# Rounding the phases of sequences 0 to 3 around the keeping of the last values

## The chip, the cores and the metric

One core of a Trainium2 chip runs the whole program. The metric is the time of one execution on the device in microseconds; the time before is the median of three runs. A profiled execution of the same program gives the trace. Its engines are TensorE (PE; PEld is its loading of weights), VectorE (DVE), ScalarE (ACT), GpSimd (POOL) and the DMA queue of SyncE (SP). Each engine runs its own queue of instructions in order, and semaphores order the engines among each other.

## The reference, cut to what matters

The model is a small language model tower over 8 sequences of 1024 tokens with 64 features: an embedding with a convolution, a two-layer recurrence of width 256 (most of the time), a feed-forward on the upper half of the tokens, an attention by phases, and a mixture of 8 experts. The change lies in the attention by phases:

```python
def encode(W1, b1, W2, b2):
    h = gelu(x @ W1 + b1, approximate=False)
    return tanh(h @ W2 + b2)
key_phase = encode(Wk1, bk1, Wk2, bk2) * freq * pi
query_phase = encode(Wq1, bq1, Wq2, bq2) * freq * pi
key_phasor = cos(key_phase) + 1j * sin(key_phase)
query_conj = cos(query_phase) - 1j * sin(query_phase)
V = x @ Wv + bv
memory = cumsum(key_phasor[..., None] * V[:, :, None, :], axis=1)
retrieved = real(sum(memory * query_conj[..., None], axis=2)) / sqrt(positions * K)
normed = (retrieved - mu) / sqrt(var + 1e-5) * ln_w + ln_b
return x + normed @ Wo + bo
```

freq is 1, 2, 4 or 8, so a phase can be several turns. Before a sine or cosine is taken, the kernel brings it to the nearest whole turn: it rounds the tanh output on a grid and subtracts the rounded value. The cosine is taken as the sine of a quarter turn less the absolute value.

## The kernel before, in words

All work is written out by hand, one list of instructions for each engine, with semaphores between them. Nothing plans the order: an engine does its instructions as they stand in its own block. Tokens lie as 8 sequences, each as 8 tiles of 128 tokens.

Around the change there are three stages:

- *Second norm, phases and values* (some 850 to 901 us of the span). For each sequence b, VectorE normalises it (second_in, second_variance, second_out), TensorE computes hidden phases, phases and values, ScalarE applies gelu and tanh. phase_tanh(b) (L1178) writes the tanh outputs of 64 key and 64 query phases into rph, a tile that has room for all 8 sequences. values_kept(b) (L1997) on VectorE takes the values of a sequence out of TensorE's bank and counts s_vr.
- *Attention* (some 901 to 985 us). On VectorE, rounded(b) is a tensor_scalar (L1991) into the tile whole and a tensor_tensor (L1992) that subtracts it from the own part of rph, and counts s_thr_r; the tile whole is one for all sequences. absolute(b) (L2018) writes one of two buffers rabs and counts s_abs; from sequence 2 on it waits until the sines of sequence b - 2 are done. ScalarE then takes four sines for a sequence: key cosines (L1231), key sines (L1236), query cosines (L1242) and query sines (L1244). TensorE turns the keys (keys, L1608), forms the scores (L1619) and the sums of keys by values (memory, L1629), and reads (read, L1643 and L1648); VectorE masks the scores (masked, L2026) and adds up the memory (L2034, L2036). ScalarE keeps what was read (attention_kept, L1259 and L1260), TensorE projects it (project_out, L1658 and L1662), and VectorE forms its variance (L2043) and adds it to the rows (add_out, L2048 to L2052).
- *Experts* (from 985 us on).

Between the first two stages stands one small side chain. VectorE's L2054 writes lnb, the normalisation's bias spread over a tile, and counts s_lnb. TensorE waits for it (after s_vr = 8) and multiplies it by the output weights in two small matmuls (L1668, L1669), ahead of keys(0). ScalarE waits for those, copies the row (L1263), and only behind this copy, in its own queue, stand the sines of sequence 0:

```python
act.wait_ge(s_row_b, 1)
act.activation(cwb[:, :], bank[6][:, D:2 * D], ACT.Copy).then_inc(s_row_k, 1)
for b in range(2):
    key_cosines(b)
```

VectorE's order before the change is: the loop over the second norm, values_kept(7), lnb (L2054), rounded(0), absolute(0), rounded(1), absolute(1), masked(0), memory(0), and then the loop over b, which for b < 6 begins with rounded(b + 2) and absolute(b + 2) (with three small blocks of the third norm and the gates ahead of them at b = 4, 6 and 7).

Of the kernel before, what the change touches and what calls it, by code (L numbers as in the profile page):

```python
# [7 lines left out]
ALU = mybir.AluOpType  # L8
# [4 lines left out]
I32 = mybir.dt.int32  # L13
# [4 lines left out]
B, T = 8, 1024  # L18
# [73 lines left out]
def build(nc, a, out, kept):  # L92
    with ExitStack() as ctx:
# [3 lines left out]
        def sem(name):  # L97
            return ctx.enter_context(nc.semaphore(name))
# [13 lines left out]
        def wide_sums(layer, s):  # L112
# [80 lines left out]
        s_kq, s_kqg, s_ph, s_th, s_thr_r, s_v, s_vr = (  # L193
            sem(n) for n in ("kq_hidden", "kq_gelu", "kq_phase", "kq_tanh", "phase_kept", "values_summed", "values_kept"))
        s_abs, s_phk, s_phi, s_s, s_sm, s_k, s_kt, s_st, s_mem, s_att, s_rt = (
            sem(n) for n in ("phases_absolute", "key_phasors", "phasors", "scores", "scores_masked", "keys_turned",
                             "keys_copied", "memory_added", "memory_summed", "attention_summed", "attention_kept"))
# [100 lines left out]
        def tokens(x):  # L298

            return x.rearrange("p (t d) -> p t d", t=TT)  # L300
# [589 lines left out]
        rph = hi_space.bitcast(F32)  # L890
# [25 lines left out]
        rabs = lo2[:, 0:2048].rearrange("p (q t) -> p q t", q=2)  # L916
# [908 lines left out]
        def _(dve):  # L1825
# [143 lines left out]
            def second_in(b):  # L1969
                dve.wait_ge(s_ytr, 5 + b // 2)  # L1970
                link(dve.tensor_tensor(tmp8[:, :, :], yw[:, span(b), :],
                                       weigh[:, span(b)].unsqueeze(2).to_broadcast([P, TT, D + 1]), ALU.mult))
                dve.tensor_tensor(xc2[:, b % 2, :, :], tmp8[:, :, :], res[:, span(b), :], ALU.add).then_inc(s_xc, 1)

            def second_variance(b):
                dve.wait_ge(s_sq, b + 1)
                dve.reduce_sum(rstd_row(b, 0), sq[:, :, :], AX.X).then_inc(s_var, 1)

            def second_out(b):
                dve.wait_ge(s_rstd, b + 1)  # L1980
                if b:
                    dve.wait_ge(s_xs, OPEN + b)
                dve.tensor_tensor(nrm[:, :, :], xc2[:, b % 2, :, 0:D], spread(rstd_row(b, 2)), ALU.mult).then_inc(s_nrm, 1)
                dve.wait_ge(s_nrm, b + 1)
                dve.tensor_tensor(res[:, span(b), :], xc2[:, b % 2, :, :], nrmw[:, :, :], ALU.add)
                norm_low(dve, b)

            def rounded(b):
                own = rph[:, b * T:(b + 1) * T]
                dve.wait_ge(s_th, 2 * b + 2)  # L1990
                link(dve.tensor_scalar(whole[:, :], own, column(GRID), column(GRID), ALU.add, ALU.subtract))  # L1991
                dve.tensor_tensor(own, own, whole[:, :], ALU.subtract).then_inc(s_thr_r, 1)  # L1992

            dve.wait_ge(s_fcb, 1)
            def values_kept(b):
                dve.wait_ge(s_v, b + 1)
                dve.tensor_scalar(vv[:, span(b), :], tokens(bank[4][:, :]), inv[:, S_V:S_V + 1], None,  # L1997
                                  ALU.mult).then_inc(s_vr, 1)
# [4 lines left out]
            for b in range(B):  # L2003
                if b + 1 < B:
                    second_variance(b + 1)
                second_out(b)
                if b + 2 < B:
                    second_in(b + 2)
                if b:
                    values_kept(b - 1)  # L2010
            values_kept(B - 1)


            def absolute(b):
                if b >= 2:
                    dve.wait_ge(s_phi, b - 1)
                dve.wait_ge(s_thr_r, b + 1)
                dve.tensor_scalar(rabs[:, b % 2, :].bitcast(I32), rph[:, b * T:(b + 1) * T].bitcast(I32), 0x7FFFFFFF, None,  # L2018
                                  ALU.bitwise_and).then_inc(s_abs, 1)

            def masked(b):
                if b >= 2:
                    dve.wait_ge(s_att, b - 1)
                for half in range(2):
                    dve.wait_ge(s_s, b * 2 + half + 1)
                    dve.tensor_tensor(sm[:, b % 2, half * 4:half * 4 + 4, :],  # L2026
                                      bank[2 + half][:, :].rearrange("p (t k) -> p t k", t=4),
                                      tri[:, :].unsqueeze(1).to_broadcast([P, 4, P]), ALU.mult).then_inc(s_sm, 1)
# [17 lines left out]
            def add_out(b):  # L2046
                own, part = res[:, span(b), 0:D], tmp8[:, :, 0:D]
                link(dve.tensor_tensor(own, own, rows(cwb[:, :]), ALU.add))  # L2048
                dve.wait_ge(s_rs, b + 1)
                dve.tensor_tensor(part, tokens(bank[7][:, :]), spread(stat[:, 7, :]), ALU.mult).then_inc(s_wor, 1)  # L2050
                dve.wait_ge(s_wor, b + 1)
                link(dve.tensor_tensor(own, own, part, ALU.add))  # L2052
# [4 lines left out]
            def third_mean(x):  # L2057
                link(dve.reduce_sum(stat[:, 0, :], res[:, span(x), 0:D], AX.X))

            def third_centre(x):  # L2060
                dve.wait_ge(s_nrm, B + x)
                dve.scalar_tensor_tensor(xc[:, :, :], spread(stat[:, 0, :]), -1.0 / D, res[:, span(x), 0:D], ALU.mult,
                                         ALU.add).then_inc(s_xc, 1)
# [10 lines left out]
            def third_low(x):  # L2074
                dve.wait_ge(s_xh, B + x + 1)
                dve.tensor_tensor(xs3_by[1], by_half(nrm[:, :, :]), xs3_by[0], ALU.subtract).then_inc(s_xs, 1)
# [12 lines left out]
            def gate_greater(x):  # L2089
                dve.wait_ge(s_rank, x + 1)  # L2090
                link(dve.tensor_tensor(gdiff[:, :, :, :], gdiff[:, :, :, :],
                                       order[:, :, :].unsqueeze(1).to_broadcast([P, TT, NE, NE]), ALU.is_gt))

            def gate_rank(x):
                link(dve.reduce_sum(grank[:, :, :], gdiff[:, :, :, :], AX.X))
                link(dve.tensor_scalar(gsel[:, :, :], grank[:, :, :], 1.5, None, ALU.is_lt))

            def gate_weights(x):
                dve.wait_ge(s_ex, x + 1)
                link(dve.tensor_tensor(gc[:, :, :], gex[:, :, :], gsel[:, :, :], ALU.mult))  # L2100
                link(dve.reduce_sum(gst[:, 1, :], gc[:, :, :], AX.X))
                link(dve.reciprocal(gst[:, 2, :], gst[:, 1, :]))
                if x:
                    dve.wait_ge(s_wgt_t, x)
                dve.tensor_tensor(gleft[:, 0:NE, :].rearrange("p e t -> p t e"), gc[:, :, :], per(gst[:, 2, :]),
                                  ALU.mult).then_inc(s_wgt, 1)

            for b in range(2):
                rounded(b)
                absolute(b)  # L2110
            masked(0)
            memory(0)
            dve.wait_ge(s_row_k, 1)
            for b in range(B):
                if b == 4:
                    third_low(0)
                elif b == 6:
                    gate_greater(0)
                    gate_rank(0)
                    gate_weights(0)  # L2120
                elif b == 7:
                    third_low(1)
                if b < B - 2:
                    rounded(b + 2)
                    absolute(b + 2)
                if b < B - 1:
                    masked(b + 1)
                if b:
                    add_out(b - 1)
                if b == 1:  # L2130
                    third_mean(0)
                    third_centre(0)
                elif b == 2:
                    third_variance(0)
                elif b == 3:
                    third_scale(0)
                    third_mean(1)
                elif b == 4:
                    third_centre(1)
                elif b == 5:  # L2140
                    third_variance(1)
                    gate_logits(0, bank[6][:, D:2 * D])
                elif b == 6:
                    third_scale(1)
                elif b == 7:
                    third_mean(2)
                    third_centre(2)
                if b < B - 1:
                    memory(b + 1)
                variance_of(b)  # L2150
# [28 lines left out]
            for n in range(slots):  # L2179
                b, e = divmod(n, NE)  # L2180
# [119 lines left out]
```

## Time and profile before

| | us |
|---|---|
| median of three runs (lowest, highest) | 1123.51 (1123.03, 1123.75) |
| profiled execution | 1123.85 |
| its span | 1122.0 |
| PE busy | 1061.1 (95%) |
| ACT busy | 769.2 (69%) |
| DVE busy | 686.4 (61%) |
| POOL busy | 147.4 (13%) |

The timeline counts in microseconds from the start of the span. A row of it has the start, the time of the instruction or of a merged group of them, the engine, the line of the program, the operation, what it writes and reads, and how many instructions the row holds. In brackets is idle time of that engine just before, and what ended it. In the table by windows, PEclk is the granted clock of TensorE as a share of the full 2.4 GHz; 0.50 is 1.2 GHz.

### The profile page before, as it was taken

How to read it: one execution, taken by the hardware profiler on the slowest of the kernel's cores; microseconds unless marked ns; L12 is line 12 of the kernel's file. 1: busy time of each engine (PE TensorE's matmuls, PEld its weight loads, DVE VectorE, ACT ScalarE, POOL GpSimd, SP SyncE). 2: the span in 40 equal slices, each digit the busy share in tenths (PEclk: the TensorE clock that was granted, in tenths of full speed). 3: DMA queues.
4: the chain of work that ended last, by engine and by line, in shares of the span. 5: the costliest groups of instructions: out<-in, count | busy, mean ns of one | idle time of the engine just before them, and what ended most of it. 6: DMA issues, size and time to landing. Idle time of an engine off the chain costs nothing.

```text
span 1122.0 us, 62678 instructions
## 1 busy us (share of the span) xinstructions
PE 1061.1 (95%) x26978; PEld 859.2 (77%) x26978; DVE 686.4 (61%) x3132; ACT 769.2 (69%) x4585; POOL 147.4 (13%) x220
## 2 busy tenths in 40 slices
PE   4799999999999999999999999999899879889998
PEld 2688899999999999999999999999744368833332
DVE  7566455555555555555555544444456758899996
ACT  1466677777767777777777776666567888667664
POOL 4300000011000100000110000000003402341320
PEclk9699999999999999999999999898699989999999
DMA  5000000000000000000000000000000000167786
GB/s 147 7 10 9 9 9 15 9 10 9 9 11 13 9 9 9 10 14 9 9 5 5 4 5 5 5 4 5 3 1 1 1 2 1 29 240 249 277 294 209
DMA packets 30642, 47.29 MB, mean 42 GB/s; under 512 B 12298, under 2 KB 21651, under 8 KB 30364
## 3 DMA queue, kind: packets, MB, share of 16 engines
q1 hardware_dynamic: 29820, 43.15, 11.5%
q8 instruction: 211, 3.46, 1.2%
q14 instruction: 67, 0.55, 0.2%
q10 hardware_dynamic: 544, 0.13, 0.1%
HBM read 40.88 MB, written 2.39 MB: 39 GB/s over the span
## 4 chain that ended last, share of the span: by engine, by line
PE 80%; DVE 9%; ACT 5%; issue 3%; DMA 2%; POOL 1%; SPq 0%; DVEq 0%; ACTq 0%; POOLq 0%
PE bank L680 44%; PE bank L777 7%; PE bank L671 5%; PE bank L760 4%; PE bank L441 3%; PE bank L540 2%; PE bank L1750 2%; PE bank L1696 2%; DMA space<-weights_kept 1%; PE bank L1437 1%; PE bank L1470 1%; PE bank L755 1%; DVE space L2159 1%; PE bank L1619 1%; PE bank L772 1%
## 5 line engine op out<-in xcount | busy, mean ns | idle before, releaser
L680 PE MATMUL bank<-space,whh_hi 128*128 128x32 f16 (+1 forms) x16384 | 574.0, 175 | 8.3 <-DVE space L808 4.4
L680 PEld LDWEIGHTS bank<-space,whh_hi 128*128 128x128 f16 x16384 | 481.9, 96 | 71.1 <-DVE space L808 8.0
L808 DVE TENSOR_TENSOR space<-h_f,space 128x16 f16<-128x16 f32 x2048 | 284.6, 176 | 365.5 <-ACT h_f L789 360.9
L789 ACT ACTIVATE h_f<-bank 128x16 f32<-128x16 f32 x2048 | 293.4, 184 | 226.4 <-PE bank L680 220.3
L795 ACT ACTIVATE space<-bank 128x16 f16<-128x16 f32 x2048 | 292.6, 184 | 1.1 <-PE bank L680 1.1
L671 PE MATMUL bank<-space,whh_lo 128*128 128x32 f16 (+1 forms) x2096 | 131.4, 177 | 0.0
L777 PE MATMUL bank<-space,wih_hi 128*128 128x32 f16 x2048 | 129.1, 177 | 0.0
L760 PE MATMUL bank<-xr,wih_hi 128*128 128x32 f16 x512 | 97.4, 190 | 0.0
L441 PE MATMUL bank<-onehot,tab 128*128 128x128 f16 x448 | 95.5, 219 | 0.5 <-DVE prepare_cur L491 0.5
L755 PE MATMUL bank<-ones,bias 128*128 128x32 bf16 x512 | 91.7, 179 | 0.0
L671 PEld LDWEIGHTS bank<-space,whh_lo 128*128 128x128 f16 x2096 | 90.1, 96 | 0.0
L777 PEld LDWEIGHTS bank<-space,wih_hi 128*128 128x128 f16 x2048 | 87.7, 96 | 0.0
L760 PE MATMUL bank<-xr,wih_lo 128*128 128x32 f16 x512 | 70.6, 193 | 0.0
L361 POOL TENSOR_SCALAR prepare_stat<-prepare_stat 128x2 f32<-128x2 f32 x28 | 6.1, 218 | 478.9 <-DVE prepare_stat L356 478.9
L777 PE MATMUL bank<-space,wih_lo 128*128 128x32 f16 x1024 | 64.5, 177 | 0.0
L772 PE MATMUL bank<-ones,bias 128*128 128x32 bf16 x512 | 52.9, 179 | 0.0
L1696 PE MATMUL bank<-xt,wx 64*128 64x512 f16 (+1 forms) x390 | 48.1, 375 | 2.3 <-ACT gel L1299 1.5
L760 PEld LDWEIGHTS bank<-xr,wih_hi 128*128 128x128 f16 x512 | 49.9, 98 | 0.0
L1299 ACT ACTIVATE space<-bank,ebias 128x1024 f32<-128x1024 f32 x31 | 33.6, 1110 | 23.1 <-PE bank L1696 23.1
L755 PEld LDWEIGHTS bank<-ones,bias 128*128 128x128 bf16 x512 | 49.2, 96 | 0.0
L760 PEld LDWEIGHTS bank<-xr,wih_lo 128*128 128x128 f16 x512 | 45.1, 96 | 0.0
L777 PEld LDWEIGHTS bank<-space,wih_lo 128*128 128x128 f16 x1024 | 43.8, 96 | 0.0
(309 smaller groups left out, 1598.9 us busy)
## 6 DMA issues: line engine op xcount, KB each, us to landing
space<-weights_kept SPq DMA_DIRECT2D x64, 512.0 KB, 7.8
space<-in_x SPq DMA_DIRECT2D x28, 129.0 KB, 3.1
out<-res SPq DMA_DIRECT2D x7, 256.0 KB, 9.8
space<-in_wrec SPq DMA_DIRECT2D x1, 768.0 KB, 4.3
space<-in_wx SPq DMA_DIRECT2D x1, 744.5 KB, 8.9
weights_kept<-wturned SPq DMA_DIRECT2D x8, 36.0 KB
whole<-weights_kept SPq DMA_DIRECT2D x8, 36.0 KB
brec<-in_brec SPq DMA_DIRECT2D x1, 260.0 KB
```

The costliest lines, as they stand in the source:

```text
L441: mm = pe.matmul(P_CONV[:, b * P:(b + 1) * P], tab[part][:, v, tap, :], onehot[:, m % 2, v, b, tap:tap + P], start=(n == 0), stop=(n == 7) ...
L671: mm = pe.matmul(own[:, m, :], w[:, k, m * P:(m + 1) * P], steps(h, k), start=False, stop=False, skip_group_check=True)
L680: mm = pe.matmul(own[:, m, 0:copies, :], w[:, k, m * P:(m + 1) * P], state[:, k, :].unsqueeze(1).to_broadcast([P, copies, B]), start=False ...
L755: pe.matmul(own, bias[:, m * P:(m + 1) * P], ones[:, 0:U * B], start=(m == 0), stop=False, skip_group_check=True)
L760: pe.matmul(own.rearrange("p s b -> p b s"), (wih0_hi, wih0_lo)[part - 1][:, m * P:(m + 1) * P], xr[:, :, n * U:(n + 1) * U], start=False, ...
L772: pe.matmul(own, bias[:, H + m * P:H + (m + 1) * P], ones[:, 0:U * B], start=(m == 0), stop=False, skip_group_check=True)
L777: pe.matmul(own, w[:, k, m * P:(m + 1) * P], h[0][:, k, at:at + U, part, :], start=False, stop=False, skip_group_check=True)
L789: act.activation(h_f[layer][:, s % 2, :, :], own, ACT.Tanh, scale=scale[layer]).then_inc(s_h[layer], 1)
L795: act.activation(h[layer][:, :, s % RINGS[layer], 0, :], own, ACT.Tanh, scale=scale[layer]).then_inc(s_hi[layer], 1)
L808: dve.tensor_tensor(h[layer][:, :, s % RINGS[layer], 1, :], h_f[layer][:, s % 2, :, :], h[layer][:, :, s % RINGS[layer], 0, :], ALU.subtra ...
L1299: act.activation(expert_at(n), banks[n % 2 * 2][:, :], ACT.Relu, bias=ebias[:, n % NE:n % NE + 1], scale=unscale[S_E1]).then_inc(s_r, 1)
L1696: mm = pe.matmul(own[:, half * 512 + at:half * 512 + at + count], wx[w][rows, W_E1 + e * HE:W_E1 + (e + 1) * HE], xt[rows, bass.ds(b * T + ...
```

## The change

In the program after, rounded(0), absolute(0), rounded(1) and absolute(1) are issued between values_kept(6) and values_kept(7). rounded(2) and rounded(3) are issued right behind values_kept(7), ahead of lnb. In the loop rounded(b + 2) is left for b + 2 of 4 or more, and absolute(b + 2) stays where it was. rounded(b) has a further wait: from sequence 1 on it waits until the subtraction of the sequence before is done, since the tile whole is shared. The same instructions are executed as before; there are seven waits more.

```diff
             def rounded(b):
                 own = rph[:, b * T:(b + 1) * T]
                 dve.wait_ge(s_th, 2 * b + 2)
+                if b:
+                    dve.wait_ge(s_thr_r, b)
                 link(dve.tensor_scalar(whole[:, :], own, column(GRID), column(GRID), ALU.add, ALU.subtract))
                 dve.tensor_tensor(own, own, whole[:, :], ALU.subtract).then_inc(s_thr_r, 1)
+
+            def absolute(b):
+                if b >= 2:
+                    dve.wait_ge(s_phi, b - 1)
+                dve.wait_ge(s_thr_r, b + 1)
+                dve.tensor_scalar(rabs[:, b % 2, :].bitcast(I32), rph[:, b * T:(b + 1) * T].bitcast(I32), 0x7FFFFFFF, None,
+                                  ALU.bitwise_and).then_inc(s_abs, 1)
...
                 if b:
                     values_kept(b - 1)
+            for b in range(2):
+                rounded(b)
+                absolute(b)
             values_kept(B - 1)
-
-
-            def absolute(b):
...
+            rounded(2)
+            rounded(3)
+
...
-            for b in range(2):
-                rounded(b)
-                absolute(b)
             masked(0)
             memory(0)
             dve.wait_ge(s_row_k, 1)
...
                 if b < B - 2:
-                    rounded(b + 2)
+                    if b + 2 >= 4:
+                        rounded(b + 2)
                     absolute(b + 2)
```

The line that writes lnb (L2054 before) is not touched; it stands between the two changed places.

## Rows read from the trace of the kernel before

**Rows 1.** The page: the chain that ended last, by engine.

```profile
PE 80%; DVE 9%; ACT 5%; issue 3%; DMA 2%; POOL 1%; SPq 0%; DVEq 0%; ACTq 0%; POOLq 0%
```

**Rows 2.** Timeline of VectorE from 894 to 927 us.

```profile
894.72 0.75 DVE L1997 TENSOR_SCALAR xr<-bank,inv 128x512 f32<-128x512 f32 x1
900.69 0.75 DVE L1997 TENSOR_SCALAR xr<-bank,inv 128x512 f32<-128x512 f32 x1 [5.22 <-PE bank L1447]
901.36 0.28 DVE L2054 TENSOR_SCALAR space<-ones,col 128x128 f32<-128x128 f32 x1
901.55 0.81 DVE L1991 TENSOR_SCALAR whole<-space,col 128x1024 f32<-128x1024 f32 x1
902.39 1.22 DVE L1992 TENSOR_TENSOR space<-space,whole 128x1024 f32<-128x1024 f32 x1
903.65 0.69 DVE L2018 TENSOR_SCALAR space<-space 128x1024 int32<-128x1024 int32 x1
904.26 0.81 DVE L1991 TENSOR_SCALAR whole<-space,col 128x1024 f32<-128x1024 f32 x1
...
916.51 0.81 DVE L1991 TENSOR_SCALAR whole<-space,col 128x1024 f32<-128x1024 f32 x1
917.35 1.22 DVE L1992 TENSOR_TENSOR space<-space,whole 128x1024 f32<-128x1024 f32 x1
918.68 0.69 DVE L2018 TENSOR_SCALAR space<-space 128x1024 int32<-128x1024 int32 x1
...
926.61 1.51 DVE L2026 TENSOR_TENSOR gel<-bank,tri 128x512 f32<-128x512 f32 x2 [0.41 <-PE bank L1619]
```

**Rows 3.** Timeline of ScalarE from 884 to 921 us.

```profile
884.08 1.10 ACT L1178 ACTIVATE space<-bank,col 128x1024 f32<-128x1024 f32 x1
...
902.73 0.22 ACT L1263 ACTIVATE space<-bank 128x64 f32<-128x64 f32 x1
904.38 1.24 ACT L1231 ACTIVATE space<-space,col 64x1024 f32<-64x1024 f32 x1 [1.42 <-DVE space L2018]
...
914.01 1.15 ACT L1244 ACTIVATE space<-space,col 64x1024 f32<-64x1024 f32 x1
...
919.41 1.24 ACT L1231 ACTIVATE space<-space,col 64x1024 f32<-64x1024 f32 x1 [3.04 <-DVE space L2018]
920.55 0.67 ACT L1259 ACTIVATE ntb<-bank,col 128x512 f32<-128x512 f32 x1
```

**Rows 4.** Timeline of TensorE from 901 to 926 us.

```profile
901.73 0.19 PE L1668 MATMUL bank<-bias,ones 128*128 128x64 bf16 x1 [1.08 <-DVE space L2054]
901.85 0.43 PE L1669 MATMUL bank<-wobd,space 64*128 64x64 f32 x2
906.83 1.97 PE L1608 MATMUL bank<-eye,space 128*128 128x128 f32 x8 [4.54 <-ACT space L1236]
909.25 3.79 PE L1619 MATMUL bank<-space 128*128 128x128 f32 x16 [0.45 <-ACT space L1244]
...
914.63 1.04 PE L1608 MATMUL bank<-eye,space 128*128 128x128 f32 x8
915.52 1.95 PE L1619 MATMUL bank<-space 128*128 128x128 f32 x16
...
918.98 0.38 PE L1648 MATMUL bank<-space,gp 128*64 128x128 f32 x2
...
925.35 2.05 PE L1619 MATMUL bank<-space 128*128 128x128 f32 x16 [1.20 <-ACT space L1244]
```

**Rows 5.** Busy time of each engine by window, attention loop; columns: window, length, engines.

```profile
926.60:951.20 24.60, 23.62 (x244) 22.11 (x242) 23.05 (x50) 19.84 (x23) 5.97 (x5) 1.00 0.00 1
```

**Rows 6.** The same view; the third number from the end is PEclk.

```profile
901.00:903.00 2.00, 0.55 (x3) 0.39 (x3) 1.97 (x4) 1.89 (x4) 0.00 (x0) 1.00 0.00 0
903.00:905.00 2.00, 0.00 (x0) 0.00 (x0) 1.97 (x3) 0.62 (x1) 0.00 (x0) 0.55 0.00 0
...
913.00:915.00 2.00, 2.00 (x19) 2.00 (x18) 0.86 (x2) 1.99 (x2) 0.00 (x0) 0.89 0.00 0
```

More of the change, by code:

```diff
@@ L2010, in _ @@
                     values_kept(b - 1)
+            for b in range(2):
+                rounded(b)
+                absolute(b)
             values_kept(B - 1)
-            def absolute(b):
[L2015 to L2019, printed above, removed]
+            rounded(2)
+            rounded(3)
             def masked(b):
```

## The prediction

> **What bounds the kernel now.** The profiled execution took 1123.85 us, 1.85 us of it outside its span of 1122.0 us; the median of the three timed runs is 1123.51 us, 0.34 us less. I count a shift of the end against the profiled execution and then apply it to the median.
>
> I read the chain of waits first. TensorE carries 80% of it, but that is an average over stages [rows 1]. The change touches 30 us of 1122, the passage from the second norm and phases into the attention loop, so only the timelines of that passage count. Four facts decide.
>
> First, VectorE has a hole: after it has kept the values of sequence 6 at 894.72 us it waits 5.22 us for TensorE's last value projection and goes on at 900.69 [rows 2].
>
> Second, VectorE then has a queue of its own: the small lnb instruction (L2054, 901.36), two rounds of 0.81 + 1.22 us with an absolute value of 0.69 us behind each, ending at 907. ScalarE's first cosine (L1231) starts at 904.38, right after the first absolute value ends at 904.34; before it lie 1.42 us of idle time [rows 2, 3].
>
> Third, a side chain goes through lnb: lnb (901.36) feeds the two row matmuls on TensorE (L1668, 901.73; L1669, ending 902.28), and ScalarE's copy of that row, L1263 at 902.73, stands ahead of the first cosine in ScalarE's queue. Before the change it is early by the 1.42 us of idle time and costs nothing [rows 3, 4].
>
> Fourth, in the loop ScalarE waits 3.04 us for the absolute value of sequence 2, which stands behind a round that starts at 916.51. Further on VectorE is busy nearly without a pause (23.05 of 24.6 us) from its first masking of sequence 2 at 926.61, and what it waited for there was scores(2) on TensorE, which in turn waited 1.20 us for ScalarE's sines (L1244) [rows 2 to 5]. Later cosines wait for VectorE too, so a shift of 926.61 goes through to the end as it is: all four engines hang on each other from there, and nothing in the last stages is tied to an absolute time.
>
> **The change part by part.**
>
> *Rounds 0 and 1 with their absolute values go into the hole.* The tanh outputs are there: that of sequence 3, the latest used ahead of the loop, starts at 884.08 and takes 1.10 us [rows 3]. A round occupies 0.84 + 1.26 us (901.55 to 902.39 to 903.65), an absolute value 0.61 (903.65 to 904.26) [rows 2]: 2.71 us for a sequence, 5.42 for two. The instruction after a keeping starts 0.67 us after it (900.69 to 901.36), so they run from 895.39 to 900.81. The keeping of the last values starts there, 0.12 us later than before. TensorE and ScalarE cover these 5.3 us. Nothing is paid, and 5.4 us of VectorE's queue behind 901.4 are gone.
>
> *Rounds 2 and 3 go between that keeping and lnb.* Here I look at what they are moved ahead of: lnb is the next instruction after them. Count on: the keeping ends its slot at 901.48. Round 2 takes 0.84 and then 1.33, because round 3 now waits for its end through two semaphores: with two waits the step behind such a subtraction is 1.33 (917.35 to 918.68), with one 1.26 [rows 2]. That is 903.65. Round 3 takes 0.84 and about 1.15 (no wait behind it; an estimate from 1.22 less the 0.08 by which instructions without a wait overlap, 903.65 to 904.26 for one of 0.69), so lnb starts at 905.64 instead of 901.36, 4.28 us late.
>
> From there: lnb's start to the end of the row matmuls was 0.92 us (902.28 less 901.36) [rows 2, 4]. They would now start at 905.64 + 0.37 = 906.01 (901.36 to 901.73), and TensorE has had nothing since 900.65 (901.73 less its 1.08 us of waiting): 5.4 us of idle time. The row of the stretch from 903 shows the granted clock falling from 2.4 to 1.2 GHz (0.55) once the engine stood still [rows 6], and eight transposes at the low level take 1.97 us against 1.04 at the high one [rows 4]. So the 0.55 us of row matmuls become at most 1.1; I take 0.25 us more. They end at 906.81 (bounds 906.56 and 907.11). ScalarE's copy follows in 0.04 and the cosine 0.25 after it (0.22 us of work and a gap of 0.03): 907.10 instead of 904.38. **The first cosine is 2.72 us late**, bounds 2.5 and 3.0. The absolute values, ready since 898 and 901, no longer matter.
>
> *What that does to sequences 0 and 1.* ScalarE's eight sines, keys_kept, TensorE's keys(0), scores(0), memory(0), keys(1) and scores(1) hang one on the other without slack, so they shift by 2.72. If TensorE's full clock came back a little earlier in this sequence, scores(1) could gain at most the 0.3 us by which it now starts (915.52) later than ScalarE's last sine of sequence 1 allows (914.01 + 1.15) [rows 3, 4].
>
> *What round 2 gives back.* Round 2 is no longer in front of absolute value 2. VectorE reaches it at 916.51 + 2.72 = 919.23 instead of 918.68, so cosine 2 starts 0.55 us late instead of 2.72. But the next instruction of ScalarE, the keeping of the attention output (L1259), needs read(0), whose last matmul ended at 918.98 + 0.38 = 919.36. ScalarE could have started at 919.40 and did at 920.55: only 1.15 us of slack in ScalarE's lateness are there to be recovered [rows 3, 4]. Read(0) now ends 2.72 later, so L1259 starts at 922.12, and the shift from here is 2.72 - 1.15 = **1.57 us**. On TensorE, project_out(0), keys(2) and scores(2) come to less (scores(2) waited 1.20 us for ScalarE), so ScalarE's sines set it.
>
> *What round 3 gives back: nothing.* It leaves a stretch in which VectorE had to wait anyway (0.41 us in front of 926.61, released by TensorE's L1619) [rows 2]. That wait becomes some 2 us longer. Rounds 4 to 7 stay where they are.
>
> *The added wait on s_thr_r.* For rounds 1 and 2 the semaphore has long arrived, for round 3 it is counted above. For rounds 4 to 7 it is a second wait in a part where VectorE sets the pace: between 0 and 0.07 us each, 0.28 in all; I take 0.08 in all, since other long instructions (0.69 us) cover such a wait. The one observation is 1.33 against 1.26 us. The Trainium skill (VectorE: DVE Perf Modes, section "The DRAIN you can't avoid") says that a semaphore after each operation costs nothing over one after the last. By it the sum is 0.15 us smaller in all; by the row, up to 0.2 larger.
>
> Sum: 2.72 - 1.15 + 0.08 = 1.65 us. On the profiled execution that is 1125.5 us, on the median **1125.2 us**.
>
> **The rivals.**
>
> *A. TensorE's full clock comes back after keys(1) and scores(1).* Before, the clock was at the high level again in the stretch from 913 (0.89 on average), just ahead of keys(1) at 914.63 [rows 4, 6]. With everything 2.7 us later and a few row matmuls alone in the middle of the idle time, it may still be low when keys(1) begins. Price: eight transposes 1.97 against 1.04, sixteen score matmuls 3.79 against 1.95 [rows 4], together 2.8 us on the chain: 1.65 + 2.8 = 4.4, so 1127.9 us, slower. It decides when the low stretch outlasts scores(0) and memory(0). For it: such short bursts did not raise the clock before. Against: keys(0) and scores(0) come just as dense as before, and they shift with the rest. The Trainium skill (TensorE: Matmul & The Clock Gate, "What's actually happening") says that the clock follows recent activity at moments that don't restart with the kernel; by that the stretch can be longer or shorter than a rigid shift makes it, which is why A has a chance at all.
>
> *B. VectorE paces the loop from its first pass on.* Then both rounds taken out of the loop would be paid back: 2.72 - 2 x 2.10 + 0.08 = -1.4, so 1122.1 us. Against it stands the 0.41 us that VectorE waited for TensorE before 926.61 [rows 2].
>
> *C. The side chain is not late*, because something else than I read orders lnb. Then the first cosine follows the row copy at 902.73 + 0.25 = 902.98, 1.40 us earlier, and the 1.15 us come on top: -2.55, so 1121.0 us. The order of the code speaks against it.
>
> *D. Slack that I did not see swallows the delay*, in the passage from attention to the experts: 1123.5 us. The dense stretch [rows 5] speaks against it.
>
> **How the numbers follow.** Forecast 0.67, A 0.14, D 0.09, B 0.06, C 0.04. A difference under 0.2% (2.25 us) can't be told from none. The forecast has its own range, 1.1 to 2.3 us and a tail, so some 0.08 of it lies over 2.25; with A that is 0.22 for slower. Faster: C and a little of B, 0.05. The rest, 0.73, is within 0.2%: a loss of 0.15% by mechanism, but too small for a verdict. The forecast's own range is 1124.5 to 1125.9; to leave no more than 0.2 outside, the range goes from 1122.9 (D in, B and C out) to 1127.0 (the shorter cases of A in).
>
> **What would show it.** Right: in the profile after, rounds 0 and 1 at 895.4 to 900.8; lnb near 905.6; the row matmuls behind it at the low clock; the copy L1263 near 906.8 and the first cosine near 907.1 with a wait on TensorE instead of VectorE; cosine 2 near 920.0; L1259 near 922.1; first masking of sequence 2 near 928.2; everything behind 1.6 us late. Wrong: a first cosine before 905, scores(1) taking over 3 us (A), or VectorE without idle time in front of the masking of sequence 2 (B).

## The result, and the profile after

The changed kernel took 1124.85 us, the median of 22 runs (1123.44 to 1126.29), against 1122.98 us for the kernel before in 22 runs of its own beside it (1122.12 to 1125.32). The ratio is 1.0016, 95% interval 1.0009 to 1.0022: 1.8 us slower (1.0 to 2.5), within the 0.2% that can hardly be told from none. The forecast was 1.65 us slower.

The profiled execution after took 1126.29 us with a span of 1124.5 us. Its passage from the norm to the attention starts 0.28 us earlier than in the one before (the last tanh, L1178, at 899.79 instead of 900.07 us), so shifts within the passage are counted from that tanh. VectorE's timeline after (rounded is now L1993 and L1994, absolute L2000, values_kept L2006, lnb L2061, masked L2033) answers to [rows 2]:

```profile
895.11 0.80 DVE L1993 TENSOR_SCALAR whole<-space,col 128x1024 f32<-128x1024 f32 x1
...
899.92 0.69 DVE L2000 TENSOR_SCALAR space<-space 128x1024 int32<-128x1024 int32 x1
900.53 0.74 DVE L2006 TENSOR_SCALAR xr<-bank,inv 128x512 f32<-128x512 f32 x1
901.19 0.80 DVE L1993 TENSOR_SCALAR whole<-space,col 128x1024 f32<-128x1024 f32 x1
902.02 1.22 DVE L1994 TENSOR_TENSOR space<-space,whole 128x1024 f32<-128x1024 f32 x1
903.36 0.81 DVE L1993 TENSOR_SCALAR whole<-space,col 128x1024 f32<-128x1024 f32 x1
904.21 1.23 DVE L1994 TENSOR_TENSOR space<-space,whole 128x1024 f32<-128x1024 f32 x1
905.35 0.28 DVE L2061 TENSOR_SCALAR space<-ones,col 128x128 f32<-128x128 f32 x1
...
917.55 0.69 DVE L2000 TENSOR_SCALAR space<-space 128x1024 int32<-128x1024 int32 x1
...
927.66 1.52 DVE L2033 TENSOR_TENSOR gel<-bank,tri 128x512 f32<-128x512 f32 x2 [1.87 <-PE bank L1619]
```

Rounds 0 and 1 with their absolute values fill the hole from 895.11 on; the last keeping starts at 900.53, 0.12 us later in the passage than before (900.69 less 0.28). Then two rounds stand in front of lnb, which starts at 905.35 instead of 901.36. In front of the masking at 927.66 VectorE now waits 1.87 us for TensorE, where it waited 0.41.

ScalarE, which answers to [rows 3]; the first row is the last tanh:

```profile
899.79 1.11 ACT L1178 ACTIVATE space<-bank,col 128x1024 f32<-128x1024 f32 x1 [0.56 <-PE bank L1527]
...
906.65 0.22 ACT L1263 ACTIVATE space<-bank 128x64 f32<-128x64 f32 x1 [4.23 <-PE bank L1669]
906.77 1.23 ACT L1231 ACTIVATE space<-space,col 64x1024 f32<-64x1024 f32 x1
...
916.39 1.14 ACT L1244 ACTIVATE space<-space,col 64x1024 f32<-64x1024 f32 x1
...
918.67 1.24 ACT L1231 ACTIVATE space<-space,col 64x1024 f32<-64x1024 f32 x1
921.58 0.69 ACT L1259 ACTIVATE ntb<-bank,col 128x512 f32<-128x512 f32 x1 [1.66 <-PE bank L1648]
```

The copy of the row, L1263, has 4.23 us of idle time in front of it, released by TensorE's row matmul, and the first cosine follows it directly. Before, ScalarE waited for the absolute value (L2018); now this wait is gone and the one for the side chain stands in its place. TensorE, which answers to [rows 4]:

```profile
905.87 0.69 PE L1669 MATMUL bank<-wobd,space 64*128 64x64 f32 x2
909.22 1.97 PE L1608 MATMUL bank<-eye,space 128*128 128x128 f32 x8 [2.66 <-ACT space L1236]
911.63 2.70 PE L1619 MATMUL bank<-space 128*128 128x128 f32 x16 [0.45 <-ACT space L1244]
...
915.68 1.04 PE L1608 MATMUL bank<-eye,space 128*128 128x128 f32 x8
917.59 2.05 PE L1619 MATMUL bank<-space 128*128 128x128 f32 x16 [0.87 <-ACT space L1244]
...
921.16 0.38 PE L1648 MATMUL bank<-space,gp 128*64 128x128 f32 x2
```

The two f32 row matmuls take 0.69 us instead of 0.43: they ran at the low clock (PEclk 0.50 from 905 to 907). The sixteen score matmuls of sequence 0 took 2.70 us instead of 3.79, because the clock came back within them (0.50 from 911 to 913, 1.00 from 913 to 915). The last row is the end of read(0), at 921.54.

Counted from the last tanh, the first cosine comes at 6.98 us (before 4.31, so 2.67 late), the first attention output L1259 at 21.79 (before 20.48, 1.31 late). From there to the seventh L1259 the shift stays at 1.31 to 1.32 us. At the eighth something new appears. The last tanh and the last L1259 on ScalarE's timeline of the execution before:

```profile
900.07 1.11 ACT L1178 ACTIVATE space<-bank,col 128x1024 f32<-128x1024 f32 x1 [0.56 <-PE bank L1527]
...
981.87 0.69 ACT L1259 ACTIVATE ntb<-bank,col 128x512 f32<-128x512 f32 x1 [3.11 <-PE bank L1648]
```

and the last L1259 after:

```profile
984.28 0.69 ACT L1259 ACTIVATE ntb<-bank,col 128x512 f32<-128x512 f32 x1 [4.49 <-PE bank L1648]
```

TensorE's first matmuls of read(7), before:

```profile
979.86 0.51 PE L1643 MATMUL bank<-gel,xr 128*64 128x128 f32 x5 [1.20 <-issue]
```

and after:

```profile
980.89 0.51 PE L1643 MATMUL bank<-gel,xr 128*64 128x128 f32 x5 [1.20 <-issue]
```

The windows around read(7) (PEclk is the third number from the end), before:

```profile
980.00:982.00 2.00, 2.00 (x34) 1.71 (x35) 1.05 (x2) 0.13 (x1) 1.94 (x1) 1.00 0.93 274
982.00:984.00 2.00, 2.00 (x24) 1.58 (x20) 1.89 (x3) 2.00 (x4) 0.00 (x0) 1.00 0.92 350
```

and after:

```profile
980.00:982.00 2.00, 1.10 (x14) 1.14 (x16) 1.90 (x7) 0.00 (x0) 1.05 (x1) 0.82 0.85 281
982.00:984.00 2.00, 2.00 (x20) 1.84 (x16) 0.97 (x3) 0.00 (x0) 0.97 (x1) 0.50 0.81 328
984.00:986.00 2.00, 2.00 (x19) 1.12 (x18) 1.87 (x3) 1.72 (x3) 0.00 (x0) 0.83 0.95 381
```

After the change TensorE ran most of read(7) at 0.50, that is at 1.2 GHz, where it had 2.4 GHz before. Ahead of it the engine had stood idle for 1.2 us in both executions. The view names no releaser (issue); by the program and VectorE's timeline it waited for the memory sums, which end 0.1 us before read(7) starts. The clock was still full in that pause and fell some 0.4 us after the matmuls had resumed (0.78 on average from 981.0 to 981.5, 0.50 from there). First to last L1259 is 61.32 us before and 62.70 after: that fall of the clock costs 1.4 us, which is why this one execution is 2.4 us over the one before and not 1.0.

### The profile page after: what moved, and what is told of

Same layout as the page of the kernel before. It is cut to its first block, busy times and chain, and to the rows that moved or that the text cites. A ratio compares the mean times of both kernels' runs of the same rounds, so it can differ in the third digit from the quotient of the medians.

```text
span 1124.5 us, 62684 instructions
## 1 busy us (share of the span) xinstructions
PE 1060.7 (94%) x26978; PEld 860.7 (77%) x26978; DVE 688.2 (61%) x3132; ACT 770.1 (68%) x4585; POOL 146.0 (13%) x220
## 4 chain that ended last, share of the span: by engine, by line
PE 82%; DVE 9%; ACT 5%; issue 3%; POOL 1%; DMA 0%; SPq 0%; DVEq 0%; ACTq 0%; POOLq 0%
PE bank L680 44%; PE bank L777 7%; PE bank L671 5%; PE bank L760 4%; PE bank L1750 3%; PE bank L441 2%; PE bank L540 2%; PE bank L1696 2%; PE bank L1437 1%; PE bank L1470 1%; PE bank L755 1%; PE bank L772 1%; PE bank L1619 1%; DVE space L1994 1%; PE bank L426 1%
```

## The experiments

Theory L: the change loses because lnb, 4.3 us late, delays the first cosine; round 2 gives back a part, round 3 nothing. Rival K: the loss is the clock of TensorE, which fell once more. Rival W: the added waits cost it. Medians scatter: the same kernel timed twice gave 0.9969 (6 runs) and 0.9982 (12 runs), 1.5 us apart. The parts that the change leaves alone scatter as much: in the fourteen traces the last tanh starts between 898.89 and 900.45 us, and from the last L1259 to the end of the span it is 139.4 to 142.2 us. So the timelines of the passage decide beside the medians. All places are counted from the start of the last tanh, in us, in the one profiled execution of each kernel; ratios are to the kernel before, timed beside each:

| kernel | ratio (95%) | first cosine | first L1259 | last L1259 | first to last |
|---|---|---|---|---|---|
| before | | 4.31 | 20.48 | 81.80 | 61.32 |
| changed | 1.0016 (1.0009 to 1.0022) | 6.98 | 21.79 | 84.49 | 62.70 |
| changed, again | 1.0019 (1.0010 to 1.0028) | 6.98 | 21.93 | 83.24 | 61.31 |
| lnb ahead | 0.9969 (0.9956 to 0.9981) | 2.78 | 18.01 | 80.88 | 62.87 |
| lnb ahead, again | 0.9982 (0.9973 to 0.9990) | 2.78 | 17.95 | 80.79 | 62.84 |
| only rounds 0 and 1 moved | 0.9988 (0.9979 to 0.9997) | 2.79 | 18.84 | 80.15 | 61.31 |
| round 3 back | 0.9992 (0.9983 to 1.0001) | 4.52 | 19.32 | 80.64 | 61.32 |
| lnb ahead, round 3 back | 0.9985 (0.9976 to 0.9993) | 2.78 | 18.06 | 80.96 | 62.90 |
| before, lnb late | 1.0029 (1.0017 to 1.0041) | 8.14 | 23.08 | 85.64 | 62.56 |
| changed, filled at read(7) | 1.0012 (1.0003 to 1.0021) | 6.98 | 21.78 | 83.10 | 61.32 |
| before, filled at read(7) | 0.9998 (0.9988 to 1.0009) | 4.31 | 20.54 | 81.84 | 61.30 |
| lnb ahead, filled at read(7) | 0.9983 (0.9974 to 0.9992) | 2.78 | 17.62 | 78.96 | 61.34 |
| lnb ahead, filled at both | 0.9980 (0.9971 to 0.9989) | 2.78 | 17.59 | 78.94 | 61.35 |
| lnb ahead, filled at keys(0) | 0.9985 (0.9975 to 0.9995) | 2.78 | 17.58 | 79.47 | 61.89 |

**lnb ahead of rounds 2 and 3.** One line of the changed kernel moves:

```diff
             values_kept(B - 1)
+            dve.tensor_scalar(lnb[:, :], ones32[:, :], column(LN_B), None, ALU.mult).then_inc(s_lnb, 1)
             rounded(2)
             rounded(3)
...
-            dve.tensor_scalar(lnb[:, :], ones32[:, :], column(LN_B), None, ALU.mult).then_inc(s_lnb, 1)
```

> The changed kernel with one line moved: lnb is written right behind values_kept(7), ahead of rounds 2 and 3. Theory L (the late side chain through lnb costs 2.7 us at the first cosine, and only that makes the change lose): lnb near 901.5, row copy near 902.7, first cosine near 903.0 instead of 904.4 before, so 1.4 us early, and the 1.15 us of slack in front of L1259 come on top: 2.5 us under the kernel before (between 1.5 and 2.9), some 4 us under the changed kernel. Rival K (the loss comes from TensorE's clock, which fell once more in the changed kernel's profiled execution, at read(7)): moving the line changes little, still 1 to 2 us over the kernel before. Rival W (the seven added waits cost it): still slower than the kernel before.

Measured: 1119.86 against 1123.56 us, ratio 0.9969: 3.5 us less by the ratio, more than the expected 1.5 to 2.9. ScalarE's timeline of this kernel, from the last tanh on:

```profile
899.83 1.11 ACT L1178 ACTIVATE space<-bank,col 128x1024 f32<-128x1024 f32 x1 [0.56 <-PE bank L1527]
...
902.49 0.22 ACT L1263 ACTIVATE space<-bank 128x64 f32<-128x64 f32 x1
902.61 1.23 ACT L1231 ACTIVATE space<-space,col 64x1024 f32<-64x1024 f32 x1
...
915.66 1.24 ACT L1231 ACTIVATE space<-space,col 64x1024 f32<-64x1024 f32 x1 [0.86 <-DVE space L2000]
917.84 0.69 ACT L1259 ACTIVATE ntb<-bank,col 128x512 f32<-128x512 f32 x1 [0.93 <-PE bank L1648]
```

The first cosine stands 1.53 us nearer to the last tanh than before and the first L1259 2.47. That is the expected 2.5. K and W expected a loss; the sign turned with one line, though this kernel has all seven added waits and its trace has the fall of the clock at read(7) too (first to last 62.87). Theory L stands.

**Only rounds 0 and 1 moved.** Rounds 2 and 3 go back into the loop, `if b + 2 >= 4` becomes `>= 2`:

> The changed kernel with rounds 2 and 3 back in the loop; only rounds 0 and 1 with their absolute values stand in the hole, and lnb follows values_kept(7) directly. Theory L: first cosine 1.4 us early, and everything behind it shifts rigidly, 1.4 us under the kernel before (0.9 to 1.8). It is then 1.1 us over the kernel with lnb ahead and rounds 2 and 3 behind it, which is what round 2 gives back. Rival K: as far over the kernel before as the changed kernel, 1 to 2 us. Rival W: the same, since the waits are still there.

```profile
900.45 1.11 ACT L1178 ACTIVATE space<-bank,col 128x1024 f32<-128x1024 f32 x1 [0.56 <-PE bank L1527]
...
903.24 1.23 ACT L1231 ACTIVATE space<-space,col 64x1024 f32<-64x1024 f32 x1
...
918.14 1.24 ACT L1231 ACTIVATE space<-space,col 64x1024 f32<-64x1024 f32 x1 [3.04 <-DVE space L2000]
919.29 0.67 ACT L1259 ACTIVATE ntb<-bank,col 128x512 f32<-128x512 f32 x1
```

Ratio 0.9988, by it 1.3 us under before. The first cosine is as early as with lnb ahead, and the 3.04 us of waiting for absolute value 2 are back in front of 918.14. The first L1259 comes 0.83 us later than with lnb ahead (18.84 against 18.01). That is what moving round 2 is worth once lnb is not behind it. I had expected 1.1; the rest lies in scores(1), which starts 13.80 us after the last tanh here and 14.12 with lnb ahead (914.25 and 913.95 in the two timelines), 0.32 us later, and 0.83 + 0.32 is 1.15.

**Round 3 back in the loop**, round 2 still ahead of lnb (`rounded(3)` ahead of the loop deleted, `>= 4` becomes `>= 3`):

> The changed kernel with round 3 back in the loop, round 2 still ahead of lnb. Theory L: lnb is 2.1 us earlier than in the changed kernel (near 903.5), first cosine near 904.9, half a microsecond later than before the change, less 1.15 us of slack: 0.6 us under the kernel before (0 to 1.2), 2 us under the changed kernel. If instead round 3 ahead of the loop gave something back, this would lose part of it: it would be less than 1.5 us under the changed kernel. Rival K: no clear difference from the changed kernel.

```profile
899.62 1.11 ACT L1178 ACTIVATE space<-bank,col 128x1024 f32<-128x1024 f32 x1 [0.56 <-PE bank L1527]
...
904.02 0.22 ACT L1263 ACTIVATE space<-bank 128x64 f32<-128x64 f32 x1 [1.77 <-PE bank L1669]
904.14 1.23 ACT L1231 ACTIVATE space<-space,col 64x1024 f32<-64x1024 f32 x1
...
916.17 1.24 ACT L1231 ACTIVATE space<-space,col 64x1024 f32<-64x1024 f32 x1 [0.17 <-DVE space L2000]
918.94 0.69 ACT L1259 ACTIVATE ntb<-bank,col 128x512 f32<-128x512 f32 x1 [1.52 <-PE bank L1648]
```

Ratio 0.9992 (0.9983 to 1.0001), where the changed kernel has 1.0016: 2.7 us less by taking one round from in front of lnb. The first cosine is 2.46 us earlier than in the changed kernel, and L1259 2.47 (19.32 against 21.79). Against the kernel before it is 0.9 us less by the ratio and 1.16 at L1259, where 0.6 (0 to 1.2) was expected: the cosine came 0.21 us late and not half a microsecond.

**lnb ahead, round 3 back in the loop**, to see round 3's worth without its cost:

> lnb ahead of round 2, round 3 back in the loop. The prediction's step that round 3 gives nothing back: VectorE waits in front of the masking of sequence 2 in either case, so L1259 and that masking come as in the kernel with lnb ahead of rounds 2 and 3 (18.0 and 24 us after the last tanh), and the time is the same within 0.5 us. If round 3 ahead of the loop were worth something, this would be slower by up to 2.1 us.

The first masking of sequence 2 on VectorE's timeline, with lnb ahead of rounds 2 and 3:

```profile
923.92 1.52 DVE L2034 TENSOR_TENSOR gel<-bank,tri 128x512 f32<-128x512 f32 x2 [1.87 <-PE bank L1619]
```

and with round 3 back in the loop:

```profile
924.13 1.29 DVE L2033 TENSOR_TENSOR gel<-bank,tri 128x512 f32<-128x512 f32 x2
```

From the last tanh these are 24.09 and 24.36 us. With the round in the loop the 1.87 us of waiting are filled, and the masking is 0.27 us late; its two halves then follow without a gap (1.29 instead of 1.52 us), so it ends at about the same place. L1259 comes at 18.06 and 18.01. The ratios are 0.9985 and, with lnb ahead, 0.9982 timed beside it (0.9969 the first time). Round 3 ahead of the loop is worth nothing on the path.

**lnb late alone**, in the kernel before: the line that writes lnb goes behind absolute(1):

> The kernel before with one line moved: lnb is written behind absolute(1) instead of ahead of rounded(0), all rounds where they were. Theory L, the cost alone: lnb starts near 907.0 instead of 901.4 (5.6 us late, of which 1.4 fall into ScalarE's old idle time), first cosine near 908.4 instead of 904.4. Round 2 is still in the loop and shifts with the rest, so nothing is given back: 3.6 to 4.0 us over the kernel before. If the side chain did not matter: no difference.

```profile
899.40 1.11 ACT L1178 ACTIVATE space<-bank,col 128x1024 f32<-128x1024 f32 x1 [0.56 <-PE bank L1527]
...
907.42 0.22 ACT L1263 ACTIVATE space<-bank 128x64 f32<-128x64 f32 x1 [5.39 <-PE bank L1669]
907.54 1.23 ACT L1231 ACTIVATE space<-space,col 64x1024 f32<-64x1024 f32 x1
...
921.33 1.24 ACT L1231 ACTIVATE space<-space,col 64x1024 f32<-64x1024 f32 x1 [1.92 <-DVE space L2018]
922.48 0.67 ACT L1259 ACTIVATE ntb<-bank,col 128x512 f32<-128x512 f32 x1
```

Ratio 1.0029 (1.0017 to 1.0041), 3.3 us slower where 3.6 to 4.0 was expected; the first cosine is 3.83 late. But at L1259 only 2.60 are left, so "nothing is given back" was wrong by 1.2 us. TensorE's full clock came back within scores(0) (2.81 us for the sixteen matmuls, 3.79 before), memory(0) ended earlier in the sequence, and with it round 2, which follows it on VectorE, and cosine 2.

**Filled at read(7).** Five matmuls on TensorE into a free bank, whose result is not used, keep it running through the 1.2 us in front of read(7), in three kernels:

```diff
+                if b == B - 1:
+                    pe.wait_ge(s_sm, 2 * B)
+                    for i in range(5):
+                        pe.matmul(bank[2][:, :], eye16[:, :], xt[:, 0:512], start=True, stop=True,
+                                  skip_group_check=True)
                 read(b)
```

> The changed kernel with five extra matmuls of 512 columns on TensorE into a free bank, just ahead of read(7), where TensorE has 1.2 us of idle time while it waits for the memory sums; their result is not used. Rival K (the clock fell to 1.2 GHz at read(7) in the changed kernel's profiled execution and cost 1.4 us there, and such falls are a good part of the measured loss): at full clock through read(7), and 1.2 to 1.4 us over the kernel before, with less spread between runs. Theory L alone: the same 1.8 us over the kernel before as without the extra matmuls, or a little more if they hold read(7) up.

> The kernel before with the five extra matmuls ahead of read(7). Control for the clock: if falls of the clock at read(7) also happen in the kernel before, in a part of its runs, it is 0.1 to 0.5 us faster and less spread than the kernel before; if they don't, or if the extra matmuls cost something, between 0 and 0.3 us slower.

> The kernel with lnb ahead of rounds 2 and 3, with the five extra matmuls ahead of read(7). Its profiled execution without them showed a fall of the clock at read(7) and the last attention output 1.5 us later than a rigid shift. Theory K for this spot: full clock through read(7), the last L1259 80.2 to 79.3 us after the start of the last tanh, and the median equal to that of the kernel without them or up to 1.4 us lower, depending on how often the fall happened in its timed runs; against the kernel before 2.5 to 4.5 us less. If the fall costs nothing: no difference.

In the timelines the fill does what it should: first to last L1259 is 61.3 us in all four kernels that have it. Of the ten traces without it five show the fall at read(7) and 62.6 to 62.9 us. (The tenth is the kernel filled at keys(0) alone, below.) The medians don't show it: 1.0012 against 1.0016 and 1.0019, 0.9998 for the kernel before, and 0.9983 where lnb ahead alone had 0.9969 and 0.9982. The changed kernel with the fill is 1.3 us over before, where K put it, but the interval (0.3 to 2.4) holds L's 1.8 as well, and its runs spread more (1123.39 to 1127.51) and not less. With lnb ahead the fill came out at 1.9 us under before, outside the expected 2.5 to 4.5, which is a miss. One place where that execution lost time can be read. From its last L1259 to the end of the span it took 142.2 us, against 139.4 to 140.8 in the other thirteen traces (139.6 in that of lnb ahead). The view of the waits has VectorE's waits for the expert weights' DMA in that execution (us in total, times, longest):

```profile
DVE gel L2169 <- DMA space<-weights_kept: 7.9, 5, 4.0
```

and in the one of lnb ahead:

```profile
DVE gel L2164 <- DMA space<-weights_kept: 5.4, 4, 2.7
```

So VectorE waited 2.5 us more for DMAs there. Whether all of that lay on the path isn't shown. The kernel filled at both places finished its attention as early and had 4.5 us of these waits and 139.7 us to the end, so the early finish alone does not bring it about; chance is likely, and not shown.

**Filled at keys(0) as well, and there alone.** Twelve such matmuls into bank 5 behind the row matmuls:

```diff
                       skip_group_check=True).then_inc(s_row_b, 1)
+            for i in range(12):
+                pe.matmul(bank[5][:, :], eye16[:, :], xt[:, 0:512], start=True, stop=True, skip_group_check=True)
```

> The same, and twelve more extra matmuls of 512 columns behind the row matmuls, in the idle time ahead of keys(0) (2.9 us), so that TensorE keeps running. If the clock stays at 2.4 GHz, keys(0) and scores(0) take 1.0 and 2.0 us instead of 1.8 and 3.8. On the path only 0.6 us can come of it, since scores(1) then waits for ScalarE's last sine of sequence 1 (in the kernel with lnb ahead it started at 913.95, the sine ended at 913.37): 0.3 to 0.6 us less than with the fill ahead of read(7) alone. If the low clock were a main cost of this passage, it would be 2 us or more.

> lnb ahead of rounds 2 and 3, and only the twelve extra matmuls ahead of keys(0). The clock stays up through keys(0) and scores(0) as in the kernel with both fills. L1259 comes 17.6 us after the last tanh against 18.0 without: 0 to 0.6 us less than lnb ahead alone, too little to be told in the median. A gain of over 1.5 us would mean that the low clock costs more than the path says.

TensorE of the kernel filled at both places:

```profile
904.90 1.09 PE L1608 MATMUL bank<-eye,space 128*128 128x128 f32 x8 [0.20 <-ACT space L1236]
907.32 2.05 PE L1619 MATMUL bank<-space 128*128 128x128 f32 x16 [1.33 <-ACT space L1244]
...
913.28 2.05 PE L1619 MATMUL bank<-space 128*128 128x128 f32 x16 [1.31 <-ACT space L1244]
```

keys(0) takes 1.09 and scores(0) 2.05 us, both at the full clock. Nevertheless L1259 comes at 17.59 and 17.58 where the four traces with lnb ahead and no fill here have 18.01, 17.95, 18.06 and 17.62: 0.0 to 0.5 us for some 2.4 us of TensorE time saved (keys(0) and scores(0) take 3.14 us together, 5.57 with lnb ahead), since scores(1) then waits 1.31 us for ScalarE's last sine. Against the kernel filled at read(7) alone it is only 0.03 us in the traces, less than the expected 0.3 to 0.6: there keys(0) and scores(0) ran at the low clock (1.97 and 3.78 us), and scores(1) still started only 0.14 us later after the last tanh (13.74 against 13.60). In the median it can't be told (0.9980 and 0.9985, 0.9983 with the fill at read(7) alone). In the kernel filled at keys(0) alone the clock fell at another place, near 967.8 us, 1.8 us into matmuls that ran without a pause behind one of 0.79 us; the seventh L1259 came late by it, and of the pause in front of read(7) only 0.16 us were left, so that first to last grew by 0.6 us (61.89).

**Twice more.** The changed kernel and the one with lnb ahead once more:

> The changed kernel once more, for a second profiled execution. Shift of L1259 from the start of the last tanh: 21.8 us, as in the first (20.5 in the kernel before), since the order sets it. The fall of the clock at read(7) is open: if it is tied to where this kernel's TensorE idles, it is there again and the last L1259 comes 84.5 us after the last tanh; if it is chance, it may be missing and that is 83.1. Time 1.3 to 2.7 us over the kernel before.

> The kernel with lnb ahead of rounds 2 and 3 once more, since its first timing (3.5 us under the kernel before) is larger than the timelines give (2.5 us at L1259). If the timelines are right, 2.0 to 3.0 us under the kernel before, and where the clock falls at read(7) 1.5 us less than that. If something else in the kernel gives a further 1 us, 3.5 again.

```profile
982.13 0.69 ACT L1259 ACTIVATE ntb<-bank,col 128x512 f32<-128x512 f32 x1 [3.11 <-PE bank L1648]
```

The changed kernel is 1.0019 again, now with a trace in which the clock held at read(7): last L1259 at 83.24 after the last tanh, first to last 61.31. So the fall is no fixed part of the change, and the 1.4 us belong to that execution. The kernel with lnb ahead repeated at 0.9982 (2.0 us under before), so its first figure was probably high; by both its traces the order alone is worth 2.5 us at the first L1259.

## Why the prediction was right

**The cover of rounds 0 and 1** held. They took 5.42 us and cost the last keeping 0.12, both as forecast.

**lnb's lateness** was read right to 0.1 us: start at 905.35 + 0.28 = 905.63 by the clock of the execution before, forecast 905.64; end of the row matmuls 906.84, forecast 906.81. The estimate of 0.25 us for their low clock measured 0.26 (0.69 less 0.43). The first cosine was 2.67 late, forecast 2.72. Here two small errors cancel: the copy started 0.09 us after the matmuls, not 0.04, and the cosine 0.12 after the copy, not 0.25.

**What round 2 gives back** held. L1259 started 1.19 us behind the end of read(0) before (920.55 less 919.36) and 0.04 after (921.58 less 921.54): the forecast 1.15. Read(0) itself was 2.46 us late, not 2.67, with the correction that I had bounded at 0.3 us: the clock came back inside scores(0), and scores(1) waited for ScalarE only. Together L1259 gained 1.36 us on the first cosine, and 1.22 in the second trace (21.93). Cosine 2 itself I had 0.55 us late; it came 0.46 us early in the first trace, because memory(0) ended sooner, and 0.41 late in the second. It did not matter, since read(0) set L1259.

**Round 3 gives nothing back** was right: shown by the kernel with lnb ahead and round 3 back. The wait in front of the masking grew from 0.41 to 1.87 us. With round 3 taken from in front of lnb and put back in the loop the loss was gone.

**The added waits** I had put at 0.08 us. From the masking of sequence 2 to the low part of the third norm (927.66 to 953.45) it is 25.79 us, before 25.80 (926.61 to 952.41): nothing, though rounds 4 and 5 with their added waits lie in it and VectorE is busy nearly throughout. The Trainium skill (VectorE: DVE Perf Modes, "The DRAIN you can't avoid") has a semaphore behind each operation cost nothing over one behind the last; this stretch agrees. A second wait right behind what it waits for is another matter: the 1.33 us of such a step did come behind round 2 (902.02 to 903.36, 1.34), where one wait had 1.26.

**The sum** was 1.65; the timelines of two executions give 1.31 and 1.45, the medians 1.8 and 2.1 with intervals from 1.0 to 3.1. What the median has above the timelines can be falls of the clock at read(7) in a part of the runs, 1.4 us each, but the filled kernel (1.0012) does not set that apart from scatter, so it stays open. The mean clock of whole executions gives no sign of it either: 0.968 over the eleven runs of the repeated changed kernel and over the 35 of the kernel before beside them, though one fall at read(7) is too short to be seen in it. One slip in the ranges: 1.1 to 2.3 us on 1123.51 is 1124.6 to 1125.8, not 1124.5 to 1125.9.

**The rivals.** A did not happen: in both traces the clock was back before keys(1). But the clock did fall at another place, read(7), which no rival had. B is refuted by the 1.87 us. C is no course of this kernel; its price, 2.55, was met by the kernel with lnb ahead (2.47 and 2.53 in the traces). D: nothing was absorbed; from the last L1259 to the end of the span it is 140.1 us before, 140.2 and 139.5 after.

## What to carry to other kernels

Before work is pulled forward on an engine that executes in order, list every instruction between its old and its new place and who waits for each: here a 0.28 us instruction of no weight stood in that stretch, and its consumer's copy stood in front of all the sines. The same change with that one line moved gains 2 to 3.5 us by the medians (2.5 by the traces) instead of losing 1.8. And price each part by the wait it removes: round 2 removed one, round 3 lay in front of a wait that another engine ends.

## What the runs showed of the hardware

The clock can fall next to a short pause: in five traces it was at 1.2 GHz during read(7), beside a pause of 1.2 us without a matmul, and in four others it held through the same pause. One of each are executions of the same program, the changed kernel, so the order of the work alone does not decide it. By the granted clock in steps of 0.5 us, the fall came in three of the five at the end of the pause (within 0.3 us before the matmuls resumed) and in two of them 0.4 and 0.5 us after they had resumed; once, in the kernel filled at keys(0) alone, it came 1.8 us into matmuls without a pause, behind one of 0.79 us. At read(7) it costs 1.2 to 1.6 us. At the start of the attention, where the clock fell in all twelve traces without a fill there, the low clock costs between nothing and 0.5 us with lnb ahead, since ScalarE's sines are the longer chain.
